# Low parts in the step that turns, sine and cosine from one angle, up weights split in two goes

## The reference, cut to what matters

```python
x = x + self_attention_0(layernorm(x))                     # 16 heads of 32, scores times a triangle
x = x + cross_attention_0(layernorm(x), ctx)               # int8-rounded q and output projections
x = x + ffn_0(layernorm(x))       # rms, 32 heads of 64 with rotary angles, causal; rms; top 4 of 16 experts
x = x + self_attention_1(layernorm(x))                     # low-rank additions to the four weights
x = x + cross_attention_1(layernorm(x), ctx)               # 16 heads of 128, context and own keys, rotary
x = x + ffn_1(layernorm(x))       # two shared experts, top 6 of 16 experts of width 352
```

## Time and profile before

| | us |
|---|---|
| median of 3 runs | 3160.03 (3158.34 to 3161.46) |
| the profiled execution | 3160.72, its span 3159.1 |
| mean granted TensorE clock | 0.909 of full speed |
| PE busy | 2683.5 (85%) |
| PE weight loads busy | 2189.0 (69%) |
| DVE busy | 1721.4 (54%) |
| ACT busy | 1137.1 (36%) |
| POOL busy | 769.1 (24%) |

### The profile page before, as it was taken

One profiled execution on the slowest core, in us unless ns is written; L12 is line 12 of the kernel. 1 busy time (PEld: TensorE's weight loads), 2 busy tenths in 40 slices (PEclk: granted clock), 3 DMA queues, 4 the chain that ended last, 5 costly groups with the idle time before them and its releaser, 6 DMA issues. The chain is left out here.

```text
span 3159.1 us, 50176 instructions
## 1 busy us (share of the span) xinstructions
PE 2683.5 (85%) x15547; PEld 2189.0 (69%) x15548; DVE 1721.4 (54%) x3346; ACT 1137.1 (36%) x2426; POOL 769.1 (24%) x795
## 2 busy tenths in 40 slices
PE   6988778978858888969999598796999988799997
PEld 6877656757747777747777387574777767688886
DVE  3425646658845555746666446583443433566564
ACT  1112235532223322435554113473444432244442
POOL 3213100003322222532333100470000001245554
PEclk9988889989969897979999699898999997899999
DMA  4443031104341103447776341325212103366663
GB/s 149 146 132 71 18 91 59 56 17 138 111 135 49 49 13 127 138 157 212 216 201 150 96 103 34 127 85 160 77 42 80 41 10 110 107 164 156 157 160 74
DMA packets 287110, 332.99 MB, mean 105 GB/s; under 512 B 147142, under 2 KB 201878, under 8 KB 284625
## 3 DMA queue, kind: packets, MB, share of 16 engines
q1 hardware_dynamic: 216464, 253.63, 26.0%
q0 software_dynamic: 20832, 52.51, 8.4%
q10 hardware_dynamic: 49632, 24.50, 2.7%
HBM read 233.86 MB, written 96.72 MB: 105 GB/s over the span
## 5 line engine op out<-in xcount | busy, mean ns | idle before, releaser
L848 PE MATMUL e_psum<-e_up_hi,hT_hi 128*128 x672 | 246.4, 367 | 28.4 <-issue 14.7
L849 PE MATMUL e_psum<-e_up_lo,hT_hi 128*128 x672 | 238.4, 355 | 0.0
L850 PE MATMUL e_psum<-e_up_hi,hT_lo 128*128 x672 | 238.1, 354 | 0.0
L1629 DVE TENSOR_REDUCE joint_a_mx<-joint_psum 112x1 f32<-112x487 f32 x128 | 85.1, 665 | 188.6 <-PE joint_psum L1603 188.5
L132 PE MATMUL p_psum<-p_p_w_hi,hT_hi 128*128 128x512 f32 x336 | 141.5, 421 | 28.4 <-DVE p_p_w_lo L1081 28.4
L848 PEld LDWEIGHTS e_psum<-e_up_hi,hT_hi 128*128 128x128 f32 x672 | 127.9, 190 | 52.8 <-issue 40.1
L1401 POOL TENSOR_TENSOR self_a_p<-self_a_p,self_a_mx 112x448 f32<-112x448 f32 x96 | 94.5, 984 | 281.5 <-DVE self_a_mx L1458 281.5
L1492 ACT ACTIVATE self_a_p<-self_a_p 112x448 f32<-112x448 f32 x128 | 72.9, 576 | 228.4 <-POOL self_a_p L1401 177.4
L1616 PEld LDWEIGHTS joint_psum<-joint_a_v,joint_a_pt 125*112 125x112 f32 (+1 forms) x1024 | 123.3, 180 | 36.4 <-issue 31.3
L1603 PE MATMUL joint_psum<-joint_a_k,joint_a_q 128*112 128x487 f32 x256 | 130.5, 636 | 16.8 <-DMA joint_a_k<-k_all 10.8
L749 ACT ACTIVATE e_gate<-e_psum 128x352 f32<-128x352 f32 (+1 forms) x86 | 44.5, 517 | 268.4 <-PE e_psum L850 268.0
(11 more groups left out here) (500 smaller groups left out, 7327.0 us busy)
## 6 DMA issues: line engine op xcount, KB each, us to landing
e_up_raw<-in_L_ffn_w SPq DMA_DIRECT2D x64, 512.0 KB, 5.5
e_up_raw<-in_L_ffn_w SPq DMA_DIRECT2D x64, 352.0 KB, 4.4
e_dn_raw<-in_L_ffn_w SPq DMA_DIRECT2D x16, 1024.0 KB, 5.4
q_all<-p_p_t_stage ACTq DMA_DIRECT2D x56, 256.0 KB, 2.3
e_dn_raw<-in_L_ffn_w SPq DMA_DIRECT2D x16, 512.0 KB, 4.4
self_a_q<-q_all SPq DMA_DIRECT2D x8, 896.0 KB, 5.4
joint_a_q<-q_all SPq DMA_DIRECT2D x7, 896.0 KB, 5.3
front_c_c_raw<-in_ctxT POOLq DMA_DIRECT2D x8, 750.0 KB, 5.8
```

Source lines behind the costliest of these rows:

```text
L848: pe.matmul(out, lhs[0], rhs[0], start=k == 0, stop=False)
L849: pe.matmul(out, lhs[0], rhs[1], start=False, stop=False)
L850: return pe.matmul(out, lhs[1], rhs[0], start=False, stop=k == n_k - 1)
L1629: dve.tensor_reduce(mx[:, r, :], ps[0:T, s_banks[i % N_S], 0:S], AX.X, ALU.max).then_inc(mx_ready, 1)
```

## The change

Three edits. In `OutNormPart` the low parts are subtracted in the step in which PE turns (both that of `a_o` and that of h), MM and all later phases come a step earlier (for `n_g` 4, TURN stays at step 9, now with the subtraction), the stride of cross1 goes from 10 to 8 and its `gap` from 1.5 to 1.9. In `TablePart` the angle is reduced once; the cosine is the sine of pi/2 - |reduced angle|; the negated table is one instruction, not two; the order has two "t" after each "p", not three. In the expert stages DVE subtracts two of the four low parts at the end of the due tick and two at the start of the next.

```diff
 routed_expert_stage, vector
+                if item(-1) is not None:
+                    with dve.If(now.due_before != 0):
+                        split_up(now.e_before + 1, (now.e_before + 1) % 2, range(KC // 2, KC))
                 i = item(0)
...
                 if item(0) is not None:
                     with dve.If(due != 0):
-                        split_up(e + 1, (e + 1) % 2)
+                        split_up(e + 1, (e + 1) % 2, range(KC // 2))
 OutNormPart
-        SPLIT, MM, ADD = 1 + shift, 2 + shift, n_g + 2 + shift
-        NORM, RMS, TURN, LOW = ADD + 1, ADD + 2, ADD + 3, ADD + 4
+        MM, ADD = 1 + shift, n_g + 1 + shift
+        NORM, RMS, TURN = ADD + 1, ADD + 2, ADD + (4 if n_g > 1 else 3)
         one_bank = banks[0] == banks[1]
-        stride = LOW + 1 if one_bank else max(4, n_g + 1)
+        stride = TURN + 1 if one_bank else max(4, n_g + 1)
+        assert one_bank or TURN % stride >= n_g
...
-                if at == LOW:
+                if at == TURN:
                     dve.wait_ge(ht_hi_ready, b + 1)
...
-                if not quantise_in and SPLIT <= at < SPLIT + n_g:
-                    i = b * n_g + at - SPLIT
+                if not quantise_in and at < n_g:
+                    i = b * n_g + at
                     dve.wait_ge(hi_ready, i + 1)
 TablePart, vector
-                for shift, offset in ((0.0, 0.0), (0.25, np.pi / 2)):
-                    do(dve.tensor_scalar(tn, a, 1.0 / TWO_PI, shift, ALU.mult, ALU.add))
...
-                    do(dve.tensor_scalar(rd, rd, float(offset), 3.1415925, ALU.add, ALU.min))
-                    yield
-                    dve.tensor_scalar(rd, rd, -3.1415925, None, ALU.max).then_inc(red_ready, 1)
+                do(dve.tensor_scalar(tn, a, 1.0 / TWO_PI, None, ALU.mult))
...
+                dve.tensor_scalar(rd, rd, 3.1415925, -3.1415925, ALU.min, ALU.max).then_inc(red_ready, 1)
+                dve.wait_ge(red_ready, k + 1)
+                yield
+                quarter = turned[0:rows, 0:cols, :]
+                do(dve.scalar_tensor_tensor(quarter, rd, -1.0, rd, ALU.mult, ALU.max))
+                yield
+                dve.tensor_scalar(quarter, quarter, -1.0, float(np.pi / 2), ALU.mult, ALU.add).then_inc(red_ready, 1)
...
-                    do(dve.tensor_tensor(tn, sin_a, w1, ALU.mult))
-                    yield
-                    dve.tensor_scalar(sin_t[:, :, 0, :], tn, -1.0, None, ALU.mult).then_inc(made_ready, 1)
+                    dve.scalar_tensor_tensor(sin_t[:, :, 0, :], sin_a, -1.0, w1, ALU.mult, ALU.mult).then_inc(made_ready, 1)
 decoder
-                    g.run(attention_order(a, o, 16, 16, gap=1.5))
+                    g.run(attention_order(a, o, 16, 16, gap=1.9))
...
-                    g.run(["p"] * 4 + ["p", "t", "t", "t"] * (p.steps - 4))
+                    g.run(["p"] * 4 + ["p", "t", "t"] * (p.steps - 4))
```

More of the change, by code:

```diff
@@ L778, in _, with split_up @@
             order = Order(dve, dve_order)
-            def split_up(e, slot):
-                for k in range(KC):
+            def split_up(e, slot, pieces):
+                for k in pieces:
                     dve.wait_ge(up_hi_ready, e * KC + k + 1)
@@ L792, in tick @@
                 if isinstance(j, int) and j == -1:
-                    split_up(0, 0)
+                    split_up(0, 0, range(KC))
                     split_down(0, 0)
+                if item(-1) is not None:
+                    with dve.If(now.due_before != 0):
+                        split_up(now.e_before + 1, (now.e_before + 1) % 2, range(KC // 2, KC))
                 i = item(0)
@@ L1751, in __init__ @@
         y = ps[0:T, Y_BANK, :]
-        self.steps = 1 + (B - 1) * stride + LOW + 1
+        self.steps = 1 + (B - 1) * stride + TURN + 1
         self.stride, self.n_g, self.shift = stride, n_g, shift
@@ L1759, in each @@
                 for b in range(B):
-                    if 0 <= step - b * stride <= LOW:
+                    if 0 <= step - b * stride <= TURN:
                         phase(b, step - b * stride)
@@ L1901, in tensor @@
             for step in range(self.steps - 1):
-                here = [(b, step - b * stride) for b in range(B) if 0 <= step - b * stride <= LOW]
+                here = [(b, step - b * stride) for b in range(B) if 0 <= step - b * stride <= TURN]
                 for b, at in here:
@@ L1964, in __init__ @@
         pos_f = g.sb(f"{name}_pos_f", [128, W])
-        angle, turns, red = (g.sb(f"{name}_{n}", [128, W, half]) for n in ("angle", "turns", "red"))
+        angle, turns, red, turned = (g.sb(f"{name}_{n}", [128, W, half]) for n in ("angle", "turns", "red", "turned"))
         trig = g.sb(f"{name}_trig", [128, 2, W, half])
@@ L1975, in __init__ @@
         pieces = [(128, pos_tok, 0, TT, (0, 1))] + [(CT, pos_ctx, W * j, W, (1,)) for j in range(B * CCH // W)]
-        n_trig, n_table = 2 + 2 * 8, 5
+        n_trig, n_table = 12, 4
         self.steps = sum(n_trig + n_table * len(p[4]) for p in pieces) + 1
@@ L2007, in scalar @@
             for rows, _, _, cols, weights in pieces:
+                for _ in range(8):
+                    yield
+                act.wait_ge(red_ready, k + 1)
+                act.activation(trig[0:rows, 0, 0:cols, :], red[0:rows, 0:cols, :], ACT.Sin).then_inc(trig_ready, 1)
+                for _ in range(2):
+                    yield
+                act.wait_ge(red_ready, k + 2)
+                act.activation(trig[0:rows, 1, 0:cols, :], turned[0:rows, 0:cols, :], ACT.Sin).then_inc(trig_ready, 1)
+                k += 2
                 yield
                 yield
-                for kind in range(2):
-                    for _ in range(7):
-                        yield
-                    act.wait_ge(red_ready, k + 1)
-                    act.activation(trig[0:rows, kind, 0:cols, :], red[0:rows, 0:cols, :], ACT.Sin).then_inc(trig_ready, 1)
-                    k += 1
-                    yield
                 for _ in range(n_table * len(weights)):
@@ L2036, in vector @@
                 yield
-                for shift, offset in ((0.0, 0.0), (0.25, np.pi / 2)):
-                    do(dve.tensor_scalar(tn, a, 1.0 / TWO_PI, shift, ALU.mult, ALU.add))
[L2039 to L2048, removed]
-                    do(dve.tensor_scalar(rd, rd, float(offset), 3.1415925, ALU.add, ALU.min))
-                    yield
-                    dve.tensor_scalar(rd, rd, -3.1415925, None, ALU.max).then_inc(red_ready, 1)
-                    k += 1
-                    yield
-                    yield
+                do(dve.tensor_scalar(tn, a, 1.0 / TWO_PI, None, ALU.mult))
+                yield
+                do(dve.tensor_scalar(tn, tn, ROUND, ROUND, ALU.add, ALU.subtract))
+                yield
+                reuse(dve, trig_ready, k)
+                do(dve.scalar_tensor_tensor(rd, tn, -part1, a, ALU.mult, ALU.add))
+                yield
+                do(dve.scalar_tensor_tensor(rd, tn, -part2, rd, ALU.mult, ALU.add))
+                yield
+                do(dve.scalar_tensor_tensor(rd, tn, -part3, rd, ALU.mult, ALU.add))
+                yield
+                dve.tensor_scalar(rd, rd, 3.1415925, -3.1415925, ALU.min, ALU.max).then_inc(red_ready, 1)
+                dve.wait_ge(red_ready, k + 1)
+                yield
+                quarter = turned[0:rows, 0:cols, :]
+                do(dve.scalar_tensor_tensor(quarter, rd, -1.0, rd, ALU.mult, ALU.max))
+                yield
+                dve.tensor_scalar(quarter, quarter, -1.0, float(np.pi / 2), ALU.mult, ALU.add).then_inc(red_ready, 1)
+                k += 2
+                yield
+                yield
+                yield
                 dve.wait_ge(trig_ready, k)
```

## The result

3069.03 us (median of 4 runs, 3062.34 to 3069.99), against 3159.78 for the kernel before: ratio 0.9702, 95% interval 0.9684 to 0.9719. That is 91 less, where 45 was forecast; the time lies under the stated range (3086 to 3150). A later measurement of the same kernel beside the experiments gave 3069.16 and 0.9705 (0.9686 to 0.9724).

The account below looks back on a forecast made before the run. PE, 85% of the span, was taken as the bound, with DVE the pace in part of p2. Terms -29 - 26 - 16 + 11 + 15 = -45 gave 3115 from the median; range 3086 to 3150, own range 3100 to 3130.

Parts of the forecast that it names:

- Cross1, 0 forecast: Cross1: stride 8 with gap 1.9 brings all phases sooner and still fits the batch; 0 (-5 to +5).
- Self2 -29: Self2: PE's seven stands of 4.87 before L1944 go, less new waits and 1.3 coming back; -29 (-18 to -34).
- joint4 -26: Joint4: the same with seven stands of 3.37, less new waits of 8 x 1.5; -26 (-12 to -32).
- stands: PE idle before turning the second 512 columns, bank held behind DVE's ADD; seven per stage, 4.87 in self2, 3.37 in joint4.
- 16 new waits: Self2 and joint4, eight each: PE's MM behind group 3's turning waits for its low part, 1.5 (1.2 to 1.8).
- The 1.3 that was to come back: Self2, each batch: ACT's copies of the transposes queue behind its high part; 1.3 lost, +9 in the sum.
- p2 -16: p2: less DVE work on the tables (-13.8) and fewer value stores queued behind SP's wait (-2.5); -16 (-8 to -19).
- the reading that the cost goes with POOL's adds: p2: port-lock cost of 1.0 per POOL add stays, as adds stay 35; DVE part -14 and not -24.
- Self0 +11: Self0: DVE stands on the low part of h ahead of masks, ADD later, 1.6 per batch; +11 (+2 to +16).
- Self3 +15: Self3: the same order costs at least 9, up to 18 with MM partly at PE's lower clock; +15 (+3 to +18).
- Experts 0: Expert stages: two of four subtractions move across the tick's head where DVE has nothing else; 0 (-3 to +3).
- a rival priced at 42: Both expert stages: each tick's added conditional is on the path, 84 ticks at some 0.5, +42: 3157; chance 0.05.

Follow-up runs that it names:

- e5: Not a run but one of the two expert stages: 407.8 in the kernel before, 409.9 in the kernel after, difference +2.1, forecast 0.

## Why the prediction was wrong

- **Cross1, 0 forecast, -29.0.** This is the step that failed: "The order of the list is regular ... all phases come sooner and still fit". It was argued from how many steps a batch has room for, not from which lie close. With gap 1.5 the list has now one and now two attention steps between two output steps; with 1.9 it has two everywhere from step 1 on. What matters is which pairs lie close on DVE, and the runs showed it: gap alone, 29; order alone in the kernel before, 27.4. The wait of 2.14 stood in the trace of before and was not looked for. With the gap put back the kernel takes 3097.93, inside the stated range: this step alone took the result out of it.
- **Self2 -29, measured -32.0; joint4 -26, measured -27.1.** Mechanism and size right: stands gone, 16 new waits of 1.3 (1.5 forecast). The count of stands was wrong, eight in each stage and not seven: the first batch had one too, for another reason. The 1.3 that was to come back is 1.7 in self2 and 1.0 in joint4. The reason given for it, ACT's queue, was not tested; the profile names DVE's quotients.
- **p2 -16, measured -19.7.** The last table leaves 131.1 after the stage's start and not 147.7: -16.6, for -13.8. The prediction's count of DVE's work was right (60 instructions for the tables where there were 89, POOL's adds 35 in both), and their busy time fell from 77.2 to 61.9: 15.3, near the 14 of the reading that the cost goes with POOL's adds, and not 24. PE is busy 125 of 130 in the middle of the stage (700 to 830) and is now next. The tail: DVE's last wait is 10.20 for 11.21, and the cause named for it, that SP waits for the tables' stores, is wrong.
- **Self0 +11, measured +4.4.** The order of the chain is as told: DVE's low part of h starts at 356.43 after 4.65 of waiting, ADD at 359.96, 9.0 after the low part of `a_o` is out (350.94), where 10.15 was forecast and 8.5 was before. MM took 4.27 and not 5.2, as the clock rose within it (granted 0.50 from 351.0 to 353.5, 0.88 from there to 356.0). So this batch is 0.5 longer where 1.6 was forecast, mostly because MM was taken at the lower clock throughout. Over the stage the first ADD is 2.0 later and the seven distances between the ADDs are 1.8 longer together. With the low part of h later self0 took 239.5, so its place on DVE is not what costs; that it is PE's MM ahead of the scores is what is left, and was not tried by itself.
- **Self3 +15, measured +0.7** (+5.5 in a second trace). ADD comes 13.6 to 13.7 after that of the last batch four times, where it was 12.2 to 12.3 three times before: the 1.5 is there. But the fourth and the fifth distance were 13.9 each before and are 13.7 and 10.7 after, which takes most of it back; the added loss by the clock did not come.
- **Experts 0, measured +5.5** in the two traces, of which the 3.4 of e2 are clear of the spread and the 2.1 of e5 are not. The cost of a conditional in each tick was a rival priced at 42; it is an eighth of that at most.
- **Sum.** Forecast -45, profiled execution -98.4: cross1 -29, self3 -14, self0 -7, p2, self2 and joint4 -8, experts +5.5, the rest -1. The forecast came from terms for the stages that were looked into. Cross1 was priced at nothing with a bound of -5 to +5 that no row of that stage stood behind, and that is where it broke. Part of the rest is luck of the execution: in the second trace of the kernel after self3 took 243.2, 4.8 more.

## What to carry to other kernels

Where several generators share engines by a written list, don't count steps, but look which blocks of the in-order engine lie close to each other, above all where the gap isn't a whole number. Moving one block of DVE by an attention step moved PE's stand to another place, and it went only when all these pairs lay two steps apart. Before phases are shifted, try the order within one step; in self2 and joint4 it gave as much. And a short stand of PE must be priced with what runs slower behind it.

## What the runs showed of the hardware

In cross1 with gap 1.5 two waits of PE, 1.26 before 544.34 and 0.47 before 547.11, were followed by products at 2.90 for 1.56. The granted clock there, by stretch:

```profile
538.00:544.00 6.00, 5.08 (x38) 3.68 (x36) 5.40 (x17) 2.47 (x8) 1.10 (x2) 1.00 0.01 3
547.00:556.00 9.00, 8.89 (x37) 7.62 (x38) 3.42 (x11) 3.92 (x12) 0.00 (x0) 0.50 0.35 111
```
